# Graph attention and aggregation over a 4096 x 4096 adjacency: an earlier first row maximum, more of the row of t copied by ScalarE, extra products ahead on TensorE, and new tables of order

## The reference

```python
def L0(item_embs, entity_embs, adj, W, a):          # graph attention
    Wh = item_embs @ W; We = entity_embs @ W
    scores = (Wh @ a1)[:, None] + (We @ a2)[None, :]
    e = jnp.where(scores > 0, scores, 0.2 * scores)
    e = jnp.where(adj > 0, e, NEG_BIG)
    h_prime = jax.nn.softmax(e, axis=1) @ entity_embs + item_embs
    return jax.nn.elu(h_prime)
def L1(x, adj, U):                                   # aggregation, divided by the degree
    agg = jnp.einsum('ji,jd->id', adj, x)
    return jax.nn.relu(agg @ U.T / adj.sum(axis=0)[:, None])
h = jnp.maximum(_layernorm(x), 0.0);  x = x + L0(h, entity_embs, adj, W, a)
h = jnp.maximum(_layernorm(x), 0.0);  return x + L1(h, adj, U)
```

## Time and profile before

| | us |
|---|---|
| median of 3 runs | 417.88 |
| lowest and highest | 417.51, 418.51 |
| the profiled execution's own time | 418.52 |
| its span, first to last instruction | 416.3 |

### The profile page before, as it was taken

One profiled execution on the slowest core, in us unless ns is written; L12 is line 12 of the kernel. 1 busy time (PEld: TensorE's weight loads), 2 busy tenths in 40 slices (PEclk: granted clock), 3 DMA queues, 4 the chain that ended last, 5 costly groups with the idle time before them and its releaser, 6 DMA issues.

```text
span 416.3 us, 11000 instructions
## 1 busy us (share of the span) xinstructions
PE 370.8 (89%) x4797; PEld 219.9 (53%) x4797; DVE 299.5 (72%) x425; ACT 278.3 (67%) x336; POOL 119.2 (29%) x120
## 2 busy tenths in 40 slices
PE   1618876889999999999999999999999999999996
PEld 0613544644444544444544445453444447999996
DVE  6799999898986848999848997832787563307333
ACT  2303867898899998888888988898999981110000
POOL 8870487782218502103202210220111100310000
PEclk9977999999999999999999999999999999999999
DMA  9999999999999999700000000000000000001100
GB/s 168 125 107 108 111 104 110 108 108 109 106 102 103 107 104 102 80 2 0 3 0 2 2 2 2 2 2 2 2 2 2 2 2 2 2 2 31 38 20 20
DMA packets 17946, 20.85 MB, mean 50 GB/s; under 512 B 13710, under 2 KB 13774, under 8 KB 17899
## 3 DMA queue, kind: packets, MB, share of 16 engines
q0 software_dynamic: 4752, 16.90, 39.0%
q1 hardware_dynamic: 10987, 2.70, 3.6%
q10 hardware_dynamic: 2160, 0.56, 0.7%
HBM read 69.79 MB, written 1.05 MB: 170 GB/s over the span
## 4 chain that ended last, share of the span: by engine, by line
PE 56%; DVE 18%; ACT 15%; issue 9%; DMA 1%; POOL 1%; ACTq 0%; DVEq 0%; POOLq 0%
PE w L1110 17%; PE q L1088 11%; PE q L1222 10%; DVE junk L776 9%; ACT arena L606 6%; ACT q L622 6%; PE den L1118 5%; PE w L1222 4%; DVE arena L819 4%; ACT arena L610 3%; PE w L1066 2%; PE den L1222 1%; PE w L995 1%; PE den L1131 1%; PE w L1180 1%
## 5 line engine op out<-in xcount | busy, mean ns | idle before, releaser
L776 DVE CUSTOM_DVE_ANT_0 junk<-adj_sb,t_row 125x2048 uint8<-125x2048 uint8 x66 | 154.9, 2348 | 2.1
L1110 PE MATMUL w<-arena,v_sb 128*32 128x500 f32 (+3 forms) x1144 | 129.1, 513 | 0.5 <-ACT arena L610 0.5
L622 ACT ACTIVATE q<-arena,minus_b 128x1000 f32<-128x1000 f32 (+2 forms) x114 | 106.1, 931 | 9.5 <-ACT arena L606 0.4
L1088 PE MATMUL q<-bi,adj_sb 128*128 128x125 bf16 x1056 | 88.0, 220 | 18.1 <-ACT q L622 16.1
L1088 PEld LDWEIGHTS q<-bi,adj_sb 128*128 128x128 fp8e4 x1056 | 61.8, 98 | 77.1 <-ACT q L622 42.5
L606 ACT ACTIVATE arena<-q,t_col 128x1000 f32<-128x1000 f32 (+2 forms) x106 | 94.6, 903 | 1.1 <-PE q L1088 0.7
L1118 PE MATMUL den<-arena,ones 128*32 128x250 f32 (+1 forms) x960 | 76.1, 339 | 0.0
L819 DVE SCALAR_TENSOR_TENSOR arena<-arena,b_col,q 128x1000 f32<-128x1000 f32 (+2 forms) x37 | 40.8, 1103 | 41.8 <-PE q L1088 34.3
L1118 PEld LDWEIGHTS den<-arena,ones 128*32 128x32 f32 x960 | 35.6, 110 | 51.6 <-issue 48.9
L610 ACT ACTIVATE arena<-arena,t 128x1000 f32<-128x1000 f32 (+2 forms) x37 | 37.2, 1006 | 21.9 <-DVE arena L819 21.7
L1222 PE MATMUL q<-g_all,adj_sb 124*124 124x129 f16 (+2 forms) x693 | 41.2, 220 | 0.0
(11 more groups left out here) (165 smaller groups left out, 338.8 us busy)
## 6 DMA issues: line engine op xcount, KB each, us to landing
adj_sb<-in_adj_dram POOLq DMA_DIRECT2D x33, 500.0 KB, 38.4
x_sb<-in_x_dram SPq DMA_DIRECT2D x1, 928.0 KB
out_dram<-x_sb SPq DMA_DIRECT2D x9, 84.0 KB
v_sb<-n_L_gnn_entity_embs_dram SPq DMA_DIRECT2D x2, 256.0 KB, 4.8
v_sb<-n_L_gnn_entity_embs_dram ACTq DMA_DIRECT2D x2, 256.0 KB, 5.7
out_dram<-x_sb SPq DMA_DIRECT2D x3, 56.0 KB
out_dram<-x_sb SPq DMA_DIRECT2D x9, 9.0 KB
x_sb<-in_x_dram SPq DMA_DIRECT2D x1, 125.0 KB
```

The lines of the kernel that those rows point to most:

```text
L622: nc.scalar.activation(part(q[n % Q_SLOTS], nb), a_part(nb), ACT.Relu, bias=minus_b[:, c:c + 1]).then_inc(relued, 1)
L776: nc.vector.tensor_tensor_reduce(out=junk[0:R, :], in0=adj_bytes[0:R, b, half], in1=t_row[0:R, half], scale=1.0 / ONE, scalar=0.0, op0=ALU ...
L1088: last = nc.tensor.matmul(q[n % Q_SLOTS][:, bank, start:start + R], adj_sb[:, b0 + k, c * P:(c + 1) * P], bi[:, i % BI_SLOTS, k, :], start ...
L1110: last = nc.tensor.matmul(att(i)[h * D + d:h * D + d + 32, 0:(k1 - k0) * R], v_sb[:, c, d:d + 32], e[:, k0 * R:k1 * R], start=first, stop= ...
```

## The change

Four things are changed.

1. The eight copies of the row of t: ACT makes pieces 0, 2, 4, 5, 6 and 7, DVE only 1 and 3 (before: four each).
2. `guard(0, 0)` waits for ACT's first two copies and for DVE's two, that is for pieces 0 to 3, which are the half row that it reads. `guard(0, 1)` waits for the other four. `scale(0)` moves from between DVE's copies to behind `guard(0, 0)`, and `sum_s(0)` from ahead of `guard(0, 0)` to behind `guard(0, 1)`.
3. PE makes eight products of the 128 x 128 identity with itself into `z1`, which nothing reads, between the first sum of t (`t_summed` 1) and the turn of `t_min`.
4. The tables are new: three fewer tiles go DVE's way in stage 0, tile 15 of stage 1 becomes tile 16, and many of the guards and steps stand at another tile.

```diff
-    DVE_TILES = [(2, 10, 13, 17, 18, 23, 29),
-                 (9, 15, 21, 28),
+    DVE_TILES = [(11, 13, 18, 29),
+                 (9, 16, 21, 28),
...
-                   (0, 0, 1, 4, 4, 5, 7, 8, 11, 12, 13, 18, 20, 20, 21, 24),
+                   (0, 2, 2, 3, 4, 5, 7, 8, 11, 12, 14, 20, 20, 21, 24, 25),
...
-        'turn_r': (27, 27, 27, 27, None),
+        'turn_r': (28, 27, 27, 27, None),
...
+    T_ON_ACT, T_ON_DVE = (0, 2, 4, 5, 6, 7), (1, 3)
...
-            for g in range(0, NG, 2):
+            for g in T_ON_ACT:
                 act.wait_ge(shift_done, 1)
                 act.wait_ge(t_made, g + 1)
...
-            for g in range(1, NG, 2):
+            for g in T_ON_DVE:
                 dve.wait_ge(t_made, g + 1)
...
-                if g == 3:
-                    scale(0)
...
                 if b == 0 and h == 0:
-                    dve.wait_ge(t_copied_act, NG // 2)
-                    dve.wait_ge(t_copied_dve, NG // 2)
+                    dve.wait_ge(t_copied_act, 2)
+                    dve.wait_ge(t_copied_dve, len(T_ON_DVE))
+                if b == 0 and h == 1:
+                    dve.wait_ge(t_copied_act, len(T_ON_ACT))
...
-            sum_s(0)
             for b in range(*GROUPS[0]):
                 for h in range(2):
                     guard(b, h)
+                    if (b, h) == (0, 0):
+                        scale(0)
+                    if (b, h) == (0, 1):
+                        sum_s(0)
             row_shifts(0)
...
+            pe.wait_ge(t_summed, 1)
+            for k in range(8):
+                nc.tensor.matmul(z1[:, 0:P], ident[:, :], ident[:, :], start=True, stop=True)
             pe.wait_ge(t_min_done, 1)
```

More of the change, by code:

```diff
@@ L60, in graph_layers_kernel @@
     ON_ACT = [c not in DVE_TILES[i] for i, c in TILES]
-    GUARD_TILES = [(0, 5, 6, 7, 11, 12, 15, 15, 17, 20, 22, 23),
[3 rows of a table removed]
+    GUARD_TILES = [(0, 5, 6, 7, 10, 12, 14, 15, 17, 19, 22, 23),
[3 rows of a table added]
     WHEN = {
@@ L69, in graph_layers_kernel @@
         'copy_den': (None, 2, 1, 2, 1),
-        'natural': (None, 2, 4, 3, 3),
+        'natural': (None, 2, 3, 3, 3),
         'normalise': (None, 4, 6, 4, 4),
         'exp_hp': (None, 7, 7, 7, 8),
-        'elu': (None, 10, 6, 5, 8),
-        'elu_below': (None, 10, 10, 9, 9),
+        'elu': (None, 7, 6, 5, 8),
+        'elu_below': (None, 10, 9, 9, 9),
         'square': (None, 12, 11, 11, 13),
-        'spread': (None, 12, 11, 12, 14),
+        'spread': (None, 12, 11, 10, 13),
         'scale': (None, 15, 16, 15, 15),
@@ L81, in graph_layers_kernel @@
         'high': (None, 20, 19, 20, 19),
-        'sum_s': (26, 25, 25, 25, None),
-        'range': (27, 25, 27, 25, None),
-        'turn_r': (27, 27, 27, 27, None),
+        'sum_s': (26, 25, 22, 25, None),
+        'range': (27, 25, 26, 25, None),
+        'turn_r': (28, 27, 27, 27, None),
         'copy_r': (27, 27, 27, 27, None),
@@ L87, in graph_layers_kernel @@
         'copy_rows': (29, 29, 29, 29, None),
-        'centre': (19, 19, 19, None, None),
+        'centre': (20, 19, 19, None, None),
         'squared': (22, 20, 20, None, None),
-        'variance': (25, 21, 21, None, None),
+        'variance': (26, 21, 21, None, None),
         'scaled': (28, 31, 31, None, None),
[L92 to L95, removed]
+        'centre_0': (4, None, None, None, None),
+        'squared_0': (3, None, None, None, None),
+        'variance_0': (7, None, None, None, None),
+        'scaled_0': (23, None, None, None, None),
         'reduce_v': (9, None, None, None, None),
@@ L98, in graph_layers_kernel @@
         'scale_u': (9, None, None, None, None),
-        'turn_u': (10, None, None, None, None),
-        'copy_u': (15, None, None, None, None),
+        'turn_u': (8, None, None, None, None),
+        'copy_u': (16, None, None, None, None),
     }
@@ L1059, in rows @@
                 if i == 0:
-                    pe.wait_ge(t_copied_act, NG // 2)
-                    pe.wait_ge(t_copied_dve, NG // 2)
+                    pe.wait_ge(t_copied_act, len(T_ON_ACT))
+                    pe.wait_ge(t_copied_dve, len(T_ON_DVE))
                 else:
```

## The result

The changed kernel takes 419.89 us in the median of 6 runs (418.79 to 420.14), and the kernel before took 417.78 beside it (6 runs, 417.41 to 418.51). The ratio is 1.0035, with a 95% interval of 1.0021 to 1.005: it is slower. The forecast was 2.0 us less. The profiled execution took 419.94 us with a span of 417.8, where before it took 418.52 with a span of 416.3.

The account below looks back on a forecast made before the run. DVE's guards were taken to bound stage 0, ACT stage 1 and PE stages 2 to 4. 0.9 + 1.3 - 0.2 = 2.0 us off 418.52 gave 416.5, or 415.9 for the median; range 414.0 to 417.6.

Parts of the forecast that it names:

- The head, 0.9 us: Before stage 0: first guard waits only for block 0, guard(1, 0) starts at 25.2 instead of 26.07; 0.9 us gained.
- The unread products, 0: In the head: 3.2 us of PE products delay the turn of t_min by about 0.1 us; counted as 0.
- Stage 0, 1.3 us: Stage 0: three fewer scores on DVE, three more tiles on ACT's way; 1.3 us gained, bounds 0 and 1.8.
- under 5: Stage 0: ACT's idle time on scores was to fall from 6.6 us to under 5 us.
- the 1.8 us that left DVE: Stage 0: three scores of 0.60 us leave DVE, the term's upper bound if DVE bounds to the end.
- fills: End of stage 0: a mask and products ahead of the later turn_shifts fill ACT's 0.70 us wait; counted as 0.
- Stage 1, 0.2 lost: Late stage 1: one more guard ahead of row_shifts(2) delays PE's turn 0.3 us; 0.2 lost, bounds 0 and 1.
- The rival that ended on the slower side: End of stage 1: POOL stretches three guards to 3.0 us each, the late turn overpays the gain; 418.8 us, chance 0.08.
- Stages 2 to 4: Stages 2 to 4: steps move a tile or two, PE bounds; taken as 0, between 0.8 gained and 0.8 lost.
- if stage 3 grows beyond 70.7 us: Stage 3: one of the signs named beforehand that the prediction would be wrong.
- later by up to one guard, 2.3 us: Stage 3: both guards of tile 9 ahead of elu_below delay POOL and ACT's square2 by up to 2.3 us.
- The help to ACT that was foreseen in stage 2: Stage 2: the two guards that stood between two scores are spread, which helps ACT; no gain counted.

Follow-up runs that it names:

- e10_scale_first: e7_both_steps with scale(0) moved ahead of guard(0, 0), into DVE's wait for block 0; 415.84 us, ratio 0.9943 to the kernel before.
- e9_no_products: e7_both_steps without the eight unread products of the identity; 416.31 us, ratio 0.9958 to the kernel before.
- e12_stage1_old: e10_scale_first with stage 1's guards and its tile on DVE's way put back to those of before; 415.87 us, ratio 0.9952 to the kernel before.
- e6_guard10: Changed kernel with stage 3's second guard of tile 9 moved to tile 10, behind elu_below; 418.67 us, ratio 1.0004 to the kernel before.
- e5_centre17: Changed kernel with stage 2's centre at tile 17 instead of 19, ahead of both guards of tile 18; 417.78 us, ratio 0.9981 to the kernel before.
- e7_both_steps: Changed kernel with both stage 2's centre at tile 17 and stage 3's second guard of tile 9 at tile 10; 416.44 us, ratio 0.9949 to before.
- e4_head_only: The new head with all tables of the kernel before; 418.62 us, ratio 1.001 to the kernel before.
- e2_stage3_old: Changed kernel with stage 3's table alone put back (its guards and spread); 418.63 us, ratio 1.0002 to the kernel before.
- e11_old_head: e7_both_steps with the head of the kernel before, keeping the new tables with both steps mended; 416.84 us, ratio 0.9964 to the kernel before.
- e8_filler: Changed kernel with eight unread identity products on PE ahead of stage 2's mask of tile 23; 418.89 us, ratio 1.0011 to the kernel before.

## Why the prediction was wrong

**The head, 0.9 us: right.** It measured 1.02 us at `row_shifts(0)` (35.52 to 34.50), with each row where it was put: first guard behind block 0's landing (19.57, said 19.3), `weigh_h(0)` over 2 us (2.48), `guard(1, 0)` at 25.07 (said 25.2). That a guard in progress holds POOL's sum up was tried with `e10_scale_first`: the same sum takes 2.48 us issued beside a guard and 0.57 us where it has ended before the guard begins. By the Trainium skill (SBUF — State Buffer, section "Who interferes with whom") whoever issues first holds the port for its whole instruction. The trace of the changed kernel agrees in both directions: the sum of 2.48 us is issued behind the guard, and in stage 2 POOL's L427 is issued 0.02 us ahead of DVE's L698 and keeps its 1.18 us, while L698 takes 1.71 instead of 0.69.

**The unread products, 0: right.** They take 3.8 us and delay the turn of `t_min` by 0.5, not 0.1 (13.41 to 13.91), and the first guard waits for block 0 in any case. Their length, said to be 3.2 us, was scaled from rows of another width, and the wait for block 0 hid the difference. Leaving them out cost nothing (`e9_no_products`).

**Stage 0, 1.3 us: the mechanism right, the size a little high.** From `row_shifts(0)` to `copy_rows` it took 43.69 us (34.50 to 78.19), 44.61 before (35.52 to 80.13): 0.92 us. The fall of ACT's waits from 6.6 to 3.3 us was foreseen as "under 5". DVE's last step came 40.17 us behind `row_shifts(0)` before (75.69) and 39.54 now (74.04), so only 0.6 of the 1.8 us that left DVE came through there; the other 0.3 lie behind it. That the later turn "fills" ACT's wait of 0.70 us was wrong: the wait grew to 1.44, as the rows above show.

**Stage 1, 0.2 lost: right**, 59.42 against 59.22, and `e12_stage1_old` showed that the stage's own new entries cause it. The rival that ended on the slower side named this place, with 2.9 us; that mechanism did not happen.

**Stages 2 to 4: here the prediction failed.** The step is "I take 0, between 0.8 gained and 0.8 lost"; the three stages lost 1.59, 1.41 and 0.22 us, 3.2 together. The sign that the text gave for this, "if stage 3 grows beyond 70.7 us", came true at 72.1. For stage 3 the text named the cause itself, both guards of tile 9 ahead of `elu_below`, making POOL and `square2` "later by up to one guard, 2.3 us", and then priced it at nothing because PE bounds the stage. `e6_guard10` showed that this one guard costs 1.2 us (72.06 to 70.86). For stage 2 the guards of tile 18 ahead of `centre` were in the table and weren't looked at; `e5_centre17` showed that they cost 2.2 us (72.70 to 70.49), half of it the wait and half the clock. The help to ACT that was foreseen in stage 2 came too: its wait for the score of tile 15 fell from 2.42 to 0.62 us. The stage is 0.6 us shorter than before (71.11 to 70.49) once `centre` is out of the way; since `centre` then stands two tiles earlier than before, not all of the 0.6 need be the spread guards. So a stage in which PE is busy 94 to 96% of the time gives little back when other engines are faster, but with only two banks of `q` ahead it pays for a wait on ACT's way that outlasts this lead.

**The clock wasn't in the sum.** No row of before had a PE wait of 2 us in stage 2, and without the fall the stage would have lost 0.5 us instead of 1.6. The length of the wait alone doesn't tell whether a fall follows. In stage 0 PE waits 1.86 us ahead of a mask both in the changed kernel, where the clock stays up through the stage, and in `e7_both_steps`, where it falls behind it. By timelines of PE of both, and a window of `e7_both_steps` (columns as above):

```profile
63.34 0.34 PE L1097 MATMUL q<-bi,adj_sb 128*128 128x125 bf16 x3 [1.86 <-ACT q L624]
...
63.76 0.34 PE L1097 MATMUL q<-bi,adj_sb 128*128 128x125 bf16 x3 [1.86 <-ACT q L624]
...
66.00:68.00 2.00, 2.00 (x21) 0.99 (x17) 2.00 (x2) 1.91 (x5) 0.52 (x1) 0.50 0.99 102
```

There the fall costs nothing that shows: from `row_shifts(0)` to `copy_rows` `e7_both_steps` takes 43.50 us and the changed kernel 43.69. Seven of the thirteen profiled kernels that have changes (`e4`, `e7` to `e12`) have such a fall in stage 0, three of them two. What a fall costs is a matter of the stage that it falls in.

**Open.** Executions of one kernel fall into groups about 1.1 us apart, those of the changed kernel at 418.8 to 418.9 and 419.9 to 420.1. Whether the clock falls in stage 2 in each of them isn't known: the fall is in all three profiles with a wait of 2.04 to 2.05 us there (the changed kernel, `e2_stage3_old`, `e6_guard10`) and in no other profile's stage 2, but the groups also show in kernels without it. The 0.22 us of stage 4 don't come from its one new entry (`spread`): `e4_head_only` has all tables of before and takes 71.32 us there, `e11_old_head` has the old head and takes 71.34. The 0.2 us of stage 3 are missing in just these two (70.66 and 70.65) and in the kernel before; in all other traces DVE starts L858 0.23 us late behind its own reciprocal, with nothing between. Either step needs some other part of the change, and its cause stays open.

## What to carry to other kernels

In programs whose order is written out by hand, go through every moved entry and ask, on the engine that it moves, which small step now stands behind one more long instruction, and who waits for that step; a stage bound by one engine is no reason to price this at zero, since the others may be late only by the lead that the buffers give (here two banks). Where the bound engine's idle time is 2.6 us, that is the limit of the gain, and no limit of the loss. And an idle gap that an instruction has anyway, as DVE's wait for block 0, is the place for the short step that another engine needs: moving `scale(0)` there brought 0.5 to 0.6 us in the medians.

## What the runs showed of the hardware

- One wait of 2.05 us on PE, in a stage in which PE was busy 94% of the time, was followed by 3.4 us at the lower level of its clock (1.2 GHz; 0.51 and 0.52 in the windows), in all three profiles that have it. A wait of 1.14 us in stage 3 and one of 0.92 in stage 2 were not. The fall cost 1.1 us, and with eight products of the identity in the gap it was missing. In stage 0 one and the same wait of 1.86 us was followed by a fall in five profiles (`e7` to `e10`, `e12`) and not in the changed kernel, so these lengths are no threshold.
- The hold between DVE and POOL goes both ways. DVE's difference L698 took 1.71 us where POOL's sum had been issued just ahead (186.19 against 186.21) and 0.69 without. POOL's L427 took 2.48 us beside a guard and 0.57 without.
- In the head the granted clock of the windows doesn't tell PE's pace. It reads 1.00 up to 20 us in every profile, but the sixteen passes of the eight products took 3.79 us in the head (10.34) and 2.05 us in stage 2 of `e8_filler` (189.45), also at 1.00. The products that spread t took 0.22 us each from 14.4 us on in `e7_both_steps` and still 0.31 us at 15.2 in `e10_scale_first`, behind the same eight products. So these didn't bring the faster pace at the same time in each execution, and what sets it isn't shown.
